# Two context attentions repacked: heads by threes with maxima, denominators and linear bias in spare rows, in a two-batch transformer kernel on Trainium2

## The reference

```python
# layer 0: attention to a context of 77 tokens, masked
q, k, v = split(x @ Wq.T + bq), split(ctx @ Wk.T + bk), split(ctx @ Wv.T + bv)
s = einsum('bhqd,bhkd->bhqk', q, k) / sqrt(8);  s = where(mask == 0, -1e9, s)
x = layernorm chain of (x + softmax(s) @ v @ Wo.T + bo)
# layer 0, second block: self-attention (512 by 512), then a mixture of 8 experts:
y = x + moe(layernorm(x))          # idx = argmax(gate); y[idx]: 128 -> 512 -> 128
# layer 1: attention to the same context, with a linear bias in the distance
s = q k^T / sqrt(8) - slope[h] * abs(key - token - (77 - 512))
# layer 1, second block: router score, the 256 best tokens go through 128 -> 512 -> 128
```

## Time and profile before

| what | value |
|---|---|
| median of 3 runs | 802.9 us (802.57 to 803.81) |
| the profiled execution | 804.56 us, span 802.8 us |
| PE busy | 693.4 us, 86% of the span |
| DVE, ACT, POOL busy | 390.3, 298.0, 73.3 us |
| mean granted PE clock | 0.956 |

### The profile page before, as it was taken

One profiled execution on the slowest core, in us unless ns is written; L12 is line 12 of the kernel. 1 busy time (PEld: TensorE's weight loads), 2 busy tenths in 40 slices (PEclk: granted clock), 3 DMA queues, 4 the chain that ended last, 5 costly groups with the idle time before them and its releaser, 6 DMA issues.

```text
span 802.8 us, 12214 instructions
## 1 busy us (share of the span) xinstructions
PE 693.4 (86%) x4696; PEld 367.4 (46%) x4696; DVE 390.3 (49%) x909; ACT 298.0 (37%) x353; POOL 73.3 (9%) x78
## 2 busy tenths in 40 slices
PE   0887999987999999599798589899999799998965
PEld 0633332334763333489444433333333378984434
DVE  1625843646326422570614865786643442135067
ACT  0231354541334346232135233535656522212533
POOL 5105400110001000100100100100000110000010
PEclk9995999999999999599989799999999989999998
DMA  6400000003200000140000000000000032200000
GB/s 185 168 0 1 1 1 1 1 1 101 67 2 0 1 1 1 37 131 15 1 1 1 27 1 1 1 1 1 1 1 2 0 118 78 83 1 1 2 0 27
DMA packets 16223, 21.34 MB, mean 27 GB/s; under 512 B 3971, under 2 KB 9027, under 8 KB 15912
## 3 DMA queue, kind: packets, MB, share of 16 engines
q1 hardware_dynamic: 15304, 18.92, 7.7%
q10 hardware_dynamic: 864, 1.64, 0.6%
HBM read 19.50 MB, written 1.05 MB: 26 GB/s over the span
## 4 chain that ended last, share of the span: by engine, by line
PE 72%; DVE 16%; ACT 5%; issue 3%; SPq 2%; POOL 1%; DMA 1%; POOLq 0%; DVEq 0%
PE pair L852 11%; PE pair L862 7%; PE pair L840 6%; PE pair L913 6%; PE pair L713 5%; PE pair L925 5%; PE pair L820 5%; PE pair L766 3%; DVE nm L1088 3%; PE pair L808 3%; PE pair L799 3%; ACT probs L684 3%; DVE negmax L1039 2%; PE pair L791 2%; PE pair L934 2%
## 5 line engine op out<-in xcount | busy, mean ns | idle before, releaser
L1088 DVE TENSOR_REDUCE nm<-pair 128x2 f32<-128x1024 f32 x128 | 153.4, 1223 | 131.2 <-PE pair L840 130.7
L684 ACT ACTIVATE probs<-pair 128x1024 f32<-128x1024 f32 x128 | 127.0, 1024 | 95.3 <-PE pair L840 51.6
L840 PE MATMUL pair<-k,q 32*128 32x512 f32 x512 | 125.3, 646 | 5.7 <-ACT k L660 2.6
L852 PE MATMUL pair<-q,k 32*128 32x512 f32 x512 | 120.8, 635 | 4.7 <-ACT probs L684 3.5
L615 POOL TENSOR_TENSOR rstd<-vareps,small 128x4 f32<-128x4 f32 x24 | 24.8, 1033 | 677.1 <-DVE vareps L1021 677.1
L668 ACT ACTIVATE probs<-pair 103x1024 f32<-103x1024 f32 x48 | 46.5, 1020 | 64.8 <-PE pair L808 64.7
L862 PE MATMUL pair<-probs,vx 128*32 128x512 f32 x512 | 67.8, 604 | 0.5 <-ACT probs L684 0.5
L852 PEld LDWEIGHTS pair<-q,k 32*128 32x128 f32 x512 | 36.3, 184 | 64.5 <-issue 32.3
L1039 DVE TENSOR_REDUCE negmax<-pair 128x8 f32<-128x616 f32 x64 | 47.4, 793 | 33.8 <-PE pair L791 33.1
L913 PE MATMUL pair<-zT,w 128*128 (+1 forms) x352 | 61.1, 301 | 0.0
L913 PEld LDWEIGHTS pair<-zT,w 128*128 128x128 f32 x352 | 53.5, 192 | 2.7 <-issue 0.7
(11 more groups left out here) (170 smaller groups left out, 876.1 us busy)
## 6 DMA issues: line engine op xcount, KB each, us to landing
w<-in_w SPq DMA_DIRECT2D x44, 256.0 KB, 2.8
w<-in_w SPq DMA_DIRECT2D x2, 1024.0 KB
xa<-in_x SPq DMA_DIRECT2D x4, 256.0 KB, 3.2
out_dram<-xc SPq DMA_DIRECT2D x4, 256.0 KB, 2.4
w_sb<-in_w ACTq DMA_DIRECT2D x2, 320.0 KB, 6.4
mask_in<-in_mask SPq DMA_DIRECT2D x4, 154.0 KB, 3.9
wqk<-in_wqk ACTq DMA_DIRECT2D x1, 512.0 KB, 7.6
fw<-in_fw SPq DMA_DIRECT2D x2, 256.0 KB
```

The costliest lines, as they stand in the source:

```text
L684: ins = nc.scalar.activation(dst, src, ACT.Exp)
L840: ins = nc.tensor.matmul(one(q, k), v.q1[rows, g, qt * P:(qt + 1) * P], v.k1[rows, g, :], start=True, stop=True)
L852: ins = nc.tensor.matmul(one(q, k), v.k1[rows, g, kt * P:(kt + 1) * P], v.q1[rows, g, :], start=True, stop=True)
L1088: ins = nc.vector.tensor_reduce(heads[:, 2 * cp:2 * cp + 2, DK:DK + 1], two(q)[:], AX.X, ALU.max, negate=True)
```

## The change

Heads go by threes (`HT` = 3): five groups of three and one of one, 3 x 77 = 231 columns (`W3`) each. Each 32-row strip then holds 24 head columns and eight spare rows. Rows 24 to 26 (`MAXROW`) carry the negative maxima, added to the queries after a transpose (`rows3`, in place of `aux`); row 30 (`UNITROW`) carries 1 against the linear bias, which so needs no matmul of its own. The values get a column of ones per head, so that one matmul gives values and denominators and `dm` goes; a value step has four matmuls. Scores come in 11 units of up to 116 rows. Groups 4 and 5 share strips with others, so that queries and keys have two banks (`q` has two matmuls), a `max` step has six score matmuls in four banks and three reductions, and `heads` has a folding matmul. The bias matmuls of `up` are issued together ahead of the float32 ones. GpSimd's zeroing is split, batch 1's loads go ahead of `r_sb`, `SLOTS` is 5, and `TURNS` is another table.

```diff
-RUNS = [(0, 103), (103, 103), (205, 103)]
-RW = 103
...
+HT = 3
+W3 = HT * SC
+MAXROW, UNITROW = HT * DK, 30
+
+RW = 116
+RUNS = [0, W3 - RW]
+
+UNITS3 = [[(g, 0, g) for g in range(4)], [(g, 1, g) for g in range(4)], [(4, 0, 0), (4, 1, 2), (5, 0, 1)]]
+KEYS = [RW, RW, RW, RW, RW, SC]
...
-SLOTS = 4
+SLOTS = 5
...
-    2, 1, 1, 1, 1, 2, 3, 2, 8, 2, 1, 3, 2, 1, 9, 1, 3, 1, 21, 1, 3, 1, 8, 1, 5, 3, 3, 1, 3, 1, 3, 1, 7, 1, 2, 2,
...
+    1, 4, 5, 2, 1, 1, 9, 1, 6, 1, 2, 2, 3, 1, 2, 1, 1, 2, 13, 2, 2, 2, 1, 1, 1, 2, 1, 1, 1, 1, 1, 4, 3, 1, 3, 2,
...
             sp.dma_start(ident[:], t["ident"]).then_inc(consts, 16)
-            sp.dma_start(vmask[:], t["vmask"]).then_inc(consts_ctx, 16)
-            sp.dma_start(dm[:], t["dm"]).then_inc(consts_ctx, 16)
+            sp.dma_start(vmask[:], t["vmask"]).then_inc(consts_v, 16)
+            load(1)
             sp.dma_start(r_sb[:], t["r"].partition_broadcast(P)).then_inc(consts_self, 16)
-            load(1)
...
-            pe.wait_ge(set_up, 1)
...
+                    strips = [(g, g, 0) for g in range(4)] + [(4 + g, 2 * (x % 2) + g, W3) for g in range(2)]
+                    if a == 0:
+                        for k in range(4):
+                            n = 2 * HT if k // 2 == x % 2 else HT
+                            nc.tensor.matmul(one(q, k)[:, 0:n * SC].rearrange("p (c k) -> p c k", k=SC),
+                                             v.auxT[0:SC, cols],
+                                             eye3[:, 0:SC].unsqueeze(1).to_broadcast([SC, n, SC]),
+                                             start=True, stop=False, skip_group_check=True)
+                    for g, strip, c0 in strips:
+                        rows = slice(32 * strip, 32 * strip + 32)
+                        ins = nc.tensor.matmul(one(q, strip)[:, c0:c0 + W3], v.q3[rows, g // 4, cols],
+                                               v.kb[a][rows, g // 4], start=a == 2, stop=True, skip_group_check=True)
...
+                elif q.kind == "rows3":
+                    pe.wait_ge(dve_done[q.p], nth("V", b, "max", a, NT - 1))
+                    transposes(one(q), lambda k: v.nm[:, 0, k, :], ident[:])
+                    pe.wait_ge(dve_done[q.p], nth("V", b, "rows3", a) - 1)
+                    ins = transposes(one(q, 1), lambda k: v.nm[:, 1, k, :], ident[:])
...
-                    for k in range(2):
-                        for g in range(G):
-                            rows = slice(32 * g, 32 * g + 32)
-                            weights = v.vb[a][0:n, x, rows] if k == 0 else dm[0:n, x, :]
-                            ins = nc.tensor.matmul(one(q, k)[rows], weights, v.probs[0:n, slots[g // 2], g % 2, :],
-                                                   start=x == 0, stop=x == 2)
+                    for k in range(4):
+                        g, r, _ = UNITS3[x][min(k, len(UNITS3[x]) - 1)]
+                        n, at = KEYS[g], min(k, len(UNITS3[x]) - 1)
+                        ins = nc.tensor.matmul(one(q, x // 2)[32 * k:32 * k + 32], v.vb[a][0:n, r, g],
+                                               v.probs[0:n, slots[at // 2], at % 2, :], start=x != 1, stop=x != 0)
...
+                    for k in range(NT):
+                        ins = nc.tensor.matmul(one(q, 1)[:, k * FOLD:(k + 1) * FOLD], v.strips2[:, 1, k * P:(k + 1) * P],
+                                               fold[:], start=True, stop=True, skip_group_check=True)
...
                                              v.hotT[0:HOT_ROWS, bass.ds(tile * P, P)], start=f == 0, stop=False,
                                              skip_group_check=True)
+                        for f in range(NF):
+                            cols = slice(f * P, (f + 1) * P)
                             ins = nc.tensor.matmul(dst[:, cols], w1[:, n % W1_SLOTS, i % 2, cols], v.zsT[:, bass.ds(tile * P, P)], start=False, stop=True,
...
+                    nc.vector.tensor_copy(twice[:, :, 2:4], twice[:, :, 0:2]).then_inc(dve_done[q.p], 1)
+                    dve.wait_ge(pe_done[q.p], q.count["T"])
+                    ins = nc.vector.tensor_tensor(v.q3, v.q3, two(q)[:], ALU.add)
```

384 lines of the change are left out of this document (212 added, 172 removed), and 23 rows, old and new, of tables (BANKS, TAKES, TURNS).

## The result

The changed kernel takes 746.6 us (median of 4 runs, 745.5 to 748.8), the kernel before 802.9. The ratio is 0.930, with a 95% interval of 0.928 to 0.932. The prediction was 780 us with a range of 762 to 797: the direction was right, the gain of 56 us was two and a half times the 23 that I gave it, and the time lies outside the range.

The account below looks back on a forecast made before the run. PE, busy 86% of the span, was taken as the bound. Its -24.5 us, 85% let through, gave -21; with DVE +3.3, start -4, moe_rows +2 and tail -1 the sum was -21 us: 780 us, range 762 to 797.

Parts of the forecast that it names:

- inner gaps: Time without PE work between start and tail, when neither batch has work ready for PE: about 73 us.
- Rival 3: Turns fitting the shorter steps close 15 us of gaps and the start gives 8: about 764 us, chance 0.17.
- rival 2: New turns place work badly; late inputs idle PE, which then runs at half clock: 807 us, chance 0.08.
- PE's sum, -24.5: Net change in PE's work over all changed steps, from value steps to up: 24.5 us less.
- the maxima steps: PE's max steps: saved bias against a second score round, sum 0, between 7 us less and 6 more.
- the folds at the upper price: Fold matmuls in heads, priced as 128-column float32 matmuls at 0.23 us each: 3.1 us more.
- I let 85% through: Share of PE's saved work taken to reach the run time, near its 86% busy time: -21 us.
- The start, -4: Batch 1's loads ahead of r_sb and dm let batch 0's norm start sooner: 4 us less, bounds 0 and 8.
- `moe_rows`, +2: Batch 1's first exponentials would wait for moe_rows, whose last long copy ends at 90.4: 1 to 6 us, taken as 2.
- DVE, +3.3: Three reductions per max step for two: 9.8 us more DVE work, a third of it, 3.3 us, in the run time.
- The tail, -1: Batch 3 ends alone: some 9 us gained, 8 of batch 2's PE work moved ahead of the tail; 1 us less.
- Rival 1: Gaps eat the gain: DVE sets the maxima steps' pace, up gains nothing; about 800 us, chance 0.10.

Follow-up runs that it names:

- e2: The kernel before with the changed kernel's TURNS, all else as before: 781.4 us, ratio 0.972.
- e17: e1 with 9 unread bf16 matmuls put in three PE waits ahead of the low-clock stretch near the end: 788.0 us, ratio 0.979.
- e1: The changed kernel with the TURNS of the kernel before, all else as changed: 804.4 us, ratio 0.998.
- e5: The changed kernel with the old table in the first part only, up to batch 2's first queries: 761.5 us, ratio 0.944.
- e9: The changed kernel with the old table in the middle only, from batch 2's first queries to batch 3's place: 772.1 us, ratio 0.959.
- e6: The changed kernel with the old table in the last part only, from batch 3's place on: 765.3 us, ratio 0.948.
- e7: The changed kernel with each of the four matmuls of a context-attention value step issued twice: 760.6 us, ratio 0.943.
- e8: The changed kernel with the old start: GpSimd clears everything first, batch 1's input loads behind r_sb, later constants wait for the clearing: 748.0 us, ratio 0.928.
- e4: The changed kernel with four slots of probs for each batch instead of five: 745.5 us, ratio 0.927.
- e14: e6 with 9 unread bf16 matmuls in three PE waits ahead of the low-clock stretch: 750.6 us, ratio 0.930.
- e13: The changed kernel with 70 unread bf16 matmuls ahead of eight PE waits (60 to 75 and 395 to 418 us): 747.4 us, ratio 0.927.
- e3: The changed kernel with the matmuls of an up item in their old order, constant part and weights in turn: 756.4 us, ratio 0.941.
- e10: e6 with 9 unread fp32 matmuls in three PE waits ahead of the low-clock stretch: 762.6 us, ratio 0.947.
- e15: e6 with 10 unread bf16 matmuls ahead of batch 2's first exponential step of the last attention, within the low-clock stretch: 757.1 us, ratio 0.938.
- e16: The kernel before with only the order within an up item changed, four constant matmuls and then four with weights: 797.6 us, ratio 0.989.
- e18: The changed kernel with 20 unread bf16 matmuls ahead of the last four PE waits: 741.8 us, ratio 0.923.

## Why the prediction was wrong

**The step that failed** is the sentence on the table: "their effect on the 73 us of inner gaps I can't read from the old trace", with a lean of 2 us for it. The table alone is worth 21.6 us (e2) and decides whether the steps are worth 35 (781.4 to 746.6), 15 (e17) or nothing (e1). Rival 3 had turns that close 15 us of gaps, at 764 us with a chance of 0.17, and rival 2 had turns that place work badly, at 0.08. Both mechanisms showed up, and larger than I had them. The first is what happened, with the gain spread over all three parts of the table (e5, e9, e6); the second, waits that "cost twice", is part of what the old table does to the new steps. That the direction came out right is in part luck: under the old table, from whose trace the prices were read, the same steps gain nothing (e1).

**PE's sum, -24.5.** In the four traces, PE's busy time for the same steps varies with the low time. From e2 to the changed kernel, at low times of 61 and 58 us, it falls by 20.9 us. That is the best measure of the new steps' work (3 us less low time are worth up to 1.5 of it), 3.6 less than I had. Exponential steps of 2.03 us and not 1.85 make 12 x 0.18 = 2.2 of the gap and transposes of 0.90 us and not 1.06 go 1.3 the other way, so that 2.7 us stay unexplained. The value steps (20.0 for 21), the maxima steps, the folds at the upper price and `up` were right. The lower bound for the maxima steps, 7 less, was added up wrongly: a second round of 0.05 us gives 11 less by the same prices. The 0 that went into the sum doesn't rest on it.

**"I let 85% through."** Idle time did not swallow any of e7's added work, and from e2 to the changed kernel it fell as well, by 14.4 us (97.0 to 82.6). A share below one for all of PE's work was the wrong form: in e7 it passes whole, and the clock adds or takes several us.

**The start, -4.** The first query came 6.0 us (old table) or 7.3 us (new) sooner. The size was too small and the cause another: not the order of loads and clearing (e8, 1.4 us), but, by the traces, the stall of SP, which is gone without the larger transfers. What it is worth at the end no run separates.

**`moe_rows`, +2.** Not there. **The fifth slot:** nothing (e4). **DVE, +3.3:** the instructions took what I said (404.8 us busy, forecast 410). The reductions do hold PE's `rows3` transposes (waits in us, times, longest), but I have no run that separates this from the table. The changed kernel:

```profile
PE pair L742 <- DVE nm L1091: 10.9, 5, 5.2
```

**The tail, -1.** From batch 3's last values to the end it is 31.4 us (from 713.05) and was 36.7 (from 766.11): 5.3 less, where I had 9. What batch 2's moved work takes ahead of it, 8 in my sum, no run separates. The whole last part gives 3.2 us by the table, and 10.8 by both together.

**Rival 1** is refuted: DVE takes 14.5 us more and the kernel gained more than PE's sum. I had also put the page's rule too strongly: the Trainium skill, "TensorEngine Tiling (Array Packing)", under "PSUM Bottleneck", says only that emptying PSUM may become the limit.

**What stays open.** Of the 23.1 us that the table alone takes off the span, 12.4 are idle time and 10.7 PE's busy time. Under the old table the new steps lose 4.6 us in the middle part, with PE at a mean clock of 0.94 there, 0.97 in the changed kernel. That those low stretches too come from short waits is likely, but no run filled them. Nor do I know why PE's busy time falls by these 10.7 us with the same 4696 matmuls, when 10 us less low time account for 5 at most. Which property of the new order closes the gaps of the first and the middle part was not looked into either.

## What to carry to other kernels

A static order of steps and the steps' lengths are one thing: here the old table hid the whole gain of faster steps. So price them together, or run the new steps under both tables before judging either. Where a PE that is nearly full takes steps of two streams, keep independent work to put between the last short dependent steps of both; that is how the new order differs where the low stretch was (e6). If that can't be had, a few bf16 matmuls that nothing reads, ahead of waits of under 1 us, can be worth seven times their length (e14), and nothing in other places (e13): measure each. And read low time run by run before you explain a difference of 5 us, since it moved by over 20 us between runs of one kernel (e3, e10, e15, e16).

## What I had not expected of the hardware

Behind three waits of 0.78, 0.78 and 0.69 us within 6 us, and one of 1.09, PE ran at 1.2 GHz for 33 us in which it was busy for 32.3. Filling the three with 2 us of matmuls removed the stretch (e6, e14; e1, e17), though in one execution of e10 the clock fell with the waits filled. A low clock did not end just because PE was busy again. And an fp32 matmul on all 128 rows and 512 columns took about 0.9 us (e10), a bf16 one 0.22 (e18: seven in 1.52 us).
